# Gate logits from x1 and a premade grid product, long operations spread over the steps, and a block end of nine steps, in a GRU plus two-layer mixture kernel

## The chip, the core and the metric

The kernel runs on one core of a Trainium2 chip. A core has TensorE (PE), VectorE (DVE), ScalarE (ACT), GpSimd (POOL) and the queue of SyncE (SP), each with its own instruction stream; they meet by semaphores. The metric is the time of one execution on the device in microseconds (us), as the median of three runs.

## What is computed

A recurrence (GRU) runs over 512 time steps for a batch of four rows of width 512. Its states go through a mixture of eight LoRA experts, which gives x1. The second layer samples x1 along its width at the positions that a grid names (linear interpolation), routes each of the 2048 tokens to two of eight experts by a gate, and adds the experts' outputs to x1. Cut to what matters here:

```python
# layer 0: h_new = (1 - z) * n + z * h, step after step, then
base + einsum('ner,ne,eor->no', Ax, w_dense, lora_B) * SCALING
# layer 1, on x1 = x + layer 0
ix = (grid + 1.0) * 0.5 * (L - 1)
x0 = floor(ix);  w1 = ix - x0
x2 = (1 - w1) * x1[..., i0] + w1 * x1[..., i1]
logits = x2 @ gate_w.T + gate_b
top_vals, top_idx = top_k(logits, 2);  routing = softmax(top_vals)
for e in range(E):
    h = x2 @ w1[e].T + b1[e]
    y = x_glu * sigmoid(1.702 * x_glu) * (x_lin + 1.0)
    out = out + (y @ w2[e].T + b2[e]) * we[:, None]
```

## The kernel before

Every float32 operand of a product is split into two float16 parts, high and low, and each product is made of three matmuls (`PARTS`). ScalarE makes the high part, VectorE the low one (value times scale minus high part).

**Streams.** One recurrence step (`gru`) is a chain over the engines: PE multiplies the state's early part (L480), then its two parts (L486, L493) with `whh`; VectorE transposes and sums (L958 to L963), ScalarE takes the sigmoid, VectorE scans (L966), ScalarE takes the tanh, VectorE makes the new state (L972 to L977). The last instruction on `hs`, L977, ends the step; POOL's `keep` (L1261) copies the state away, and VectorE's next write of `hs` waits for that copy. Every engine's program is written by hand as: step, a piece of other work, step, a piece of other work. Which piece stands behind which step is what the tables at the top of the file say; no scheduler is involved.

**The parts of the program.** First a setup (weights loaded and split, input gates of the first 64 time steps). Then 128 steps whose other work is the *preparation* (`prelude`): `moe_hi` and `moe_lo` split 384 columns of expert weights per step on ScalarE and VectorE (L990), `gi_piece` makes input gates for later steps on PE (L503), `x_hi` and `x_lo` (L982) split inputs, `grid_op` makes the interpolation matrix `gm` for each batch row b and each quarter k of the width: g_d = position minus index (L1026), g_a = absolute value (L1028), ScalarE's hat function and its copy (`grid_hi`), and the low part (L1032); B x K = 16 of each. `GRID_AT` names their steps.

Then come four blocks f = 0 to 3 of 128 time steps each of the second half's work. Block f's work stands behind the recurrence steps of the next 128; the last block has no recurrence beside it (`gru_on` is false) and the same code runs without steps. A block is a *head* of `HEAD` = 30 steps, 15 expert tiles of `SLOT` = 6 steps and an *end* of 8 steps. The head, by step: LoRA products and first routing (0 to 5), base products (`base`, in pieces of `BASE_CUT`) and LoRA sums (`lora`, four calls in steps 6 and 9), x1 (L1107) and its split (L1112) in two halves, samples (`sample`, pieces of `SAMPLE_CUT`, 48 matmuls of 512 columns), the split of the samples x2 (L1119), their transpose (`turn_x2`, L543), gate logits from the transposed x2 (`gate`, L549), second routing (`route_a` to `route_c`), ranks (L556, L558), slots (L1126 to L1137), then four `scatter` calls on POOL (two indirect DMAs each, L1270) behind steps 23 to 26. At the end POOL gathers expert outputs (L1279) behind steps 122 to 125, ScalarE scales them, VectorE combines (L1166), PE transposes back and VectorE adds (L1161).

## Time and profile before

| what | us |
|---|---|
| median of 3 runs | 2033.37 (2032.92 to 2041.77) |
| profiled execution | 2053.76 |
| its span | 2051.9 |
| TensorE matmul busy | 1696.2 (83%) |
| VectorE busy | 1410.8 (69%) |
| ScalarE busy | 750.2 (37%) |
| POOL busy | 285.6 (14%) |
| mean granted TensorE clock | 0.966 |

The profiled execution is 20 us longer than the median, so a sum made on the trace is set against the execution's own time. The span is from the first to the last instruction of the trace. Busy shares are averages over parts with different limits: for 512 steps the chain of the recurrence sets the pace, in the last block the dependence of one product on the next.

### The profile page before, as it was taken

To read this page: it belongs to the slowest core of one execution; us is meant where nothing else is said; L and a number is where in the kernel's file an instruction comes from. 1 tells how busy PE (TensorE), PEld (TensorE's weight loads), DVE (VectorE), ACT (ScalarE), POOL (GpSimd) and SP (SyncE) were. 2 spreads that over 40 slices of the span, in tenths; PEclk is the share of its full clock that TensorE was granted. 3 is DMA by queue.
4 is the path that set the end of the run, shared out by engine and by line. 5 is a ranking of instruction groups with operands and counts; after the bars stand their busy time and mean duration, and the time that the engine had idled before them with its cause. 6 is when DMAs were issued, how large, how long until landed. Compare 5 with 4: busy or idle time off the path is not lost. (4 is left out here: it accounts for less than half of the span.)

```text
span 2051.9 us, 90285 instructions
## 1 busy us (share of the span) xinstructions
PE 1696.2 (83%) x38301; PEld 1095.2 (53%) x38301; DVE 1410.8 (69%) x6376; ACT 750.2 (37%) x2706; POOL 285.6 (14%) x581
## 2 busy tenths in 40 slices
PE   6777767778679999968599999978699999776995
PEld 4565555555445556545456566545456555442442
DVE  6888888887757777767677777767677777641221
ACT  5544444442323343322233343323233333322332
POOL 0111111121121111120211011120211111201001
PEclk9999999999989999999899999989899999987997
DMA  8444343422055464422265555240545464228995
GB/s 311 174 145 157 129 157 141 157 95 85 22 204 193 172 248 176 144 64 64 85 213 185 210 214 178 82 116 3 186 183 193 172 213 152 69 60 304 348 356 164
DMA packets 113621, 334.86 MB, mean 163 GB/s; under 512 B 41920, under 2 KB 42168, under 8 KB 100800
## 3 DMA queue, kind: packets, MB, share of 16 engines
q1 hardware_dynamic: 108096, 312.31, 42.8%
q0 software_dynamic: 5120, 16.78, 2.5%
q8 instruction: 299, 4.90, 1.0%
q14 instruction: 106, 0.87, 0.1%
HBM read 263.74 MB, written 65.32 MB: 160 GB/s over the span
## 5 line engine op out<-in xcount | busy, mean ns | idle before, releaser
L480 PE MATMUL bank_g<-whh,hs_early 128*32 128x256 f16 x8192 | 324.6, 279 | 257.7 <-DVE hs_early L972 247.9
L1261 POOL COPY hxs<-hs 128x32 f16<-128x32 f16 x512 | 221.7, 433 | 1519.6 <-DVE hs L977 1519.6
L727 ACT ACTIVATE rz<-pre 128x32 f32<-128x32 f32 x512 | 118.9, 232 | 804.2 <-DVE pre L960 804.2
L480 PEld LDWEIGHTS bank_g<-whh,hs_early 128*32 128x32 f16 x8192 | 173.8, 97 | 435.0 <-DVE hs_early L972 424.0
L958 DVE STREAM_TRANSPOSE xt<-bank_g 128x256 f32<-128x256 f32 x512 | 229.7, 449 | 201.8 <-PE bank_g L486 196.4
L626 PE MATMUL bank<-wm,wih 128*128 128x512 f16 x1440 | 351.1, 384 | 2.8 <-issue 1.6
L493 PE MATMUL bank_g<-whh,hs 128*32 128x128 f16 x16384 | 331.4, 222 | 6.6 <-issue 6.1
L486 PE MATMUL bank_g<-whh,hs 128*32 128x256 f16 x8192 | 321.6, 278 | 1.4 <-issue 1.1
L493 PEld LDWEIGHTS bank_g<-whh,hs 128*32 128x32 f16 x16384 | 290.5, 99 | 14.0 <-issue 10.3
L727 ACT ACTIVATE seq_h<-na 128x16 f32<-128x16 f32 x512 | 111.6, 218 | 283.2 <-DVE na L966 283.2
L486 PEld LDWEIGHTS bank_g<-whh,hs 128*32 128x32 f16 x8192 | 191.1, 98 | 43.5 <-DVE hs L977 3.3
L626 PEld LDWEIGHTS bank<-wm,wih 128*128 128x128 f16 x1440 | 126.9, 98 | 150.2 <-issue 20.9
L727 ACT ACTIVATE wih<-bank 128x512 f32<-128x512 f32 (+2 forms) x196 | 139.7, 713 | 132.5 <-PE bank L605 69.2
L972 DVE TENSOR_TENSOR_SCAN hs_early<-omz,seq_h 128x32 f16<-128x32 f32 x512 | 116.3, 227 | 103.3 <-ACT seq_h L727 102.9
L962 DVE STREAM_TRANSPOSE xt<-bank_g 128x128 f32<-128x128 f32 x512 | 157.8, 308 | 29.5 <-remote 17.7
L647 PE MATMUL bank<-wm,wih 128*128 128x512 f16 x720 | 173.1, 380 | 1.1 <-ACT wih L727 1.1
L503 PE MATMUL bank<-hxs,wih 128*128 128x256 f16 x1152 | 151.8, 278 | 18.2 <-DVE hxs L982 14.0
L960 DVE TENSOR_REDUCE pre<-xt 128x32 f32<-128x96 f32 x512 | 129.5, 253 | 17.6
L1149 DVE TENSOR_TENSOR wih<-bank,wih 128x512 f32<-128x512 f32 x60 | 41.2, 686 | 128.1 <-PE bank L622 128.1
L966 DVE TENSOR_TENSOR_SCAN na<-rz,seq_n 128x32 f32<-128x32 f32 x512 | 114.9, 224 | 18.8 <-DVE seq_n L963 0.8
L503 PEld LDWEIGHTS bank<-hxs,wih 128*128 128x128 f16 x1152 | 104.0, 99 | 44.0 <-DVE hxs L982 14.2
L727 ACT ACTIVATE xt<-gi 128x32 f32<-128x32 f32 x512 | 124.4, 243 | 0.0
(139 smaller groups left out, 1863.4 us busy)
## 6 DMA issues: line engine op xcount, KB each, us to landing
wm<-moe_split SPq DMA_DIRECT2D x60, 1536.0 KB
wm<-moe_split SPq DMA_DIRECT2D x60, 1024.0 KB
wm<-moe_split SPq DMA_DIRECT2D x60, 512.0 KB
wm<-in_w_moe SPq DMA_DIRECT2D x16, 1536.0 KB, 10.9
moe_split<-wm SPq DMA_DIRECT2D x16, 1536.0 KB, 6.4
wih<-x_rows SPq DMA_DIRECT2D x60, 256.0 KB, 7.6
y_rows<-wih SPq DMA_DIRECT2D x60, 256.0 KB, 4.9
xr<-in_x SPq DMA_DIRECT2D x16, 512.0 KB, 7.0
```

The lines of the kernel that those rows point to most:

```text
L480: mm(bank_g[0][32 * j:32 * j + 32, 0:2 * P], early_cols[:, 4 * B * k:4 * B * k + 32], whh[:, 1, k, at:at + 2 * P], start=(k == 0), stop=False)
L486: i = mm(bank_g[0][32 * j:32 * j + 32, 0:2 * P], hs_cols[:, 4 * B * k:4 * B * k + 32], whh[:, 0, k, at:at + 2 * P], start=False, stop=(k = ...
L493: i = mm(bank_g[1][32 * j:32 * j + 32, 0:P], hs_cols[:, 4 * B * k:4 * B * k + 32], whh[:, w, k, at:at + P], start=(k == 0 and w == 0), sto ...
L503: i = mm(bank[m % len(bank)][:, 0:N], wih[:, w, k, m * P:(m + 1) * P], xs[v % 2][:, a, k], start=(j == 0), stop=(j == len(GI) - 1))
L626: mm(bk[:, :], xgt[0][:, a, k], wm[:, par, at // HALF, w, up_at(at)], start=(c == 0), stop=False)
L647: mm(bank_down[:, :], yt[:, a, k], wm[:, par, 1, w, up_at(UPW + k * D)], start=(n == 0), stop=False)
L727: return nc.scalar.activation(dst, src, func, **kw)
L958: link(V.transpose(rows[:, 0:2 * K], bank_g[0][:, 0:2 * P].rearrange("p (m c) -> p m c", c=32)))
L960: V.tensor_reduce(pre[:, :, :], terms[:, 0:2 * K], AX, ALU.add).then_inc(S["rz_pre"], 1)
L962: link(V.transpose(rows[:, 2 * K:], bank_g[1][:, 0:P].rearrange("p (m c) -> p m c", c=32)))
L972: V.tensor_tensor_scan(early_scan, pairs["omz"], pairs["seq_h"], 0.0, ALU.mult, ALU.add).then_inc(S["h_hi"], 1)
L1261: Q.tensor_copy(hxs[:, par, :, :, :, col].rearrange("p s k b -> p s (k b)"), hs_new).then_inc(S["h_kept"], 1)
```

## The change

- **Gate logits.** Since x2 = x1 times the interpolation matrix G and logits = x2 times Wg, the product G times Wg can be made once. In the preparation PE transposes `gm` (`turn_grid`, 16 calls), ScalarE copies it out (`grid_out`), PE multiplies by `wgs` (`gate_grid`, 16 calls), and the result is split into `gws`. In the head `gate` then multiplies the split x1 (`x1s`) by `gws`, in steps 15 and 16. `turn_x2` and its copies go. `p_log`, `p_rank` and `p_count` move to another PSUM bank.
- **Samples.** The low part of x2 comes from PE and ScalarE instead of VectorE: `sub_hi` subtracts the high part from the bank by one matmul with `neg16`, and ScalarE copies what is left (`x2_lo`). The order of samples starts with rows 0 and 1 interleaved over k.
- **Head.** `lora`, x1, its high part and its low part each take one quarter per step (steps 7 to 10, 7 to 10, 8 to 11, 11 to 14). Second routing moves to steps 16 to 18, ranks to 19, slots to 19, expert numbers to 20, scatters to steps 20 to 23, each waiting for its own `x2_lo`. `HEAD` is 29.
- **Preparation.** The difference and absolute value of the grid become one `Abs` with a bias on ScalarE. All grid, x and other splits have hand-set steps, at most one long VectorE operation besides `moe_lo`. Input gates of the second visit start two steps later.
- **Setup.** The split of the second x piece, the split of b2, the 16-bit identity and the constants move from the setup into steps (`B2_AT`, `CONST_AT`). A one-element sigmoid (`warm`) stands at ScalarE's start.
- **Block end.** `TAIL` = 9 steps. Both pieces of the last `down` stand in the first of them. Gathers stand behind steps 121 to 124; `scaled`, `combined` and the last sum keep their steps.

The core of the diff:

```diff
-HEAD = 30
+HEAD = 29
+TAIL = 9
-SAMPLE = [(b, k, w, a) for b in range(B) for k in range(K) for w, a in PARTS]
-BASE_CUT = {2: (0, 8), 3: (8, 16), 4: (16, 24), 6: (24, 32), 7: (32, 40), 8: (40, 48)}
-SAMPLE_CUT = {11: (0, 6), 12: (6, 14), 13: (14, 22), 14: (22, 30), 15: (30, 39), 16: (39, 48)}
+SAMPLE = [(b, k, w, a) for k in range(K) for b in (0, 1) for w, a in PARTS] + \
+         [(b, k, w, a) for b in (2, 3) for k in range(K) for w, a in PARTS]
+BASE_CUT = {2: (0, 8), 3: (8, 16), 4: (16, 24), 5: (24, 26), 6: (26, 34), 7: (34, 38), 8: (38, 43), 9: (43, 48)}
+SAMPLE_CUT = {12: (0, 6), 13: (6, 12), 14: (12, 18), 15: (18, 19), 16: (19, 20), 17: (20, 27), 18: (27, 34),
+              19: (34, 41), 20: (41, 48)}
...
+GRID_START = (4, 26, 48, 70)
+X_LO = [s + q for s in (13, 21, 35, 53, 67, 89) for q in range(2)]
+GW_HI, B2_AT, B1_AT, CONST_AT = 104, 106, 110, 116
...
+            def sub_hi(f, b):
+                pe.wait_ge(S["x2_hi"], f * B + b + 1)
+                mm(bank[b][:, :], neg16[:, :], x2s[b][:, 0], start=False, stop=True, skip_group_check=True
+                   ).then_inc(S["x2_sub"], 1)
             def gate(f, b):
-                pe.wait_ge(S["x2t_out"], f * B + b + 1)
+                if b == 0:
+                    pe.wait_ge(S["x1_lo"], (f + 1) * K)
                 for j, (k, w, a) in enumerate(LOW):
-                    i = mm(p_log[:, b], xgt[b % 2][:, a, k], wgs[:, w, k], start=(j == 0), stop=(j == len(LOW) - 1))
+                    i = mm(p_log[:, b], x1s[:, a, k, b], gws[:, w, b, k], start=(j == 0), stop=(j == len(LOW) - 1))
...
             def last_down(f, i):
-                if i < 2:
-                    down(f, NT // 2, 0, 3 + i)
-                if i >= 4:
-                    b = i - 4
+                if i == 0:
+                    down(f, NT // 2, 0, 3)
+                    down(f, NT // 2, 0, 4)
+                if i >= 5:
+                    b = i - 5
...
+            def grid_abs(b, k):
+                act.wait_ge(S["grid_chain"], b * GRID_CHAIN + 2)
+                run(g_a, g_t, ACT.Abs, scale=-1.0, bias=iotf[:, k:k + 1]).then_inc(S["grid_a"], 1)
+            def x2_lo(f, b):
+                act.wait_ge(S["x2_sub"], f * B + b + 1)
+                run(x2s[b][:, 1], bank[b][:, :], ACT.Copy, scale=1 / WS).then_inc(S["x2_lo"], 1)
...
             def scatter(f, b):
                 if b == 0:
                     pool.wait_ge(S["slots_done"], f + 1)
-                    pool.wait_ge(S["x2_lo"], (f + 1) * B)
                     pool.wait_ge(S["xt_mm"], f * NT) if f else pool.wait_ge(S["zeroed"], 16 * NT)
+                pool.wait_ge(S["x2_lo"], f * B + b + 1)
```

How the order of instructions moves, at three places.

VectorE at the end of the setup, before. `whh` is the split of the recurrent weights, `xt<-bank_g` the first transpose of the first recurrence step.

```order
L1230 SCALAR_TENSOR_TENSOR whh<-wm,whh 128x4x32 x48
L982 SCALAR_TENSOR_TENSOR hxs<-xr,hxs 128x512 x2
L1236 SCALAR_TENSOR_TENSOR brow<-x1s,brow 8x512
L1238 MEMSET ones_f 128x128
L1239 MEMSET ones 128x128
L1240 MEMSET ones_as 128x128
L1241 SCALAR_TENSOR_TENSOR tri<-ones_f,idt 128x128
L1242 TENSOR_TENSOR tri<-tri,idt 128x128
L1243 COPY iott<-iote 128x8
L1244 TENSOR_SCALAR iott<-iote 128x8
L1245 TENSOR_SCALAR full<-iote 128x4
L958 STREAM_TRANSPOSE xt<-bank_g 128x256
```

The same place of the change:

```order
L1284 MEMSET ws_col 128x1
L1289 SCALAR_TENSOR_TENSOR whh<-wm,whh 128x4x32 x48
L1011 STREAM_TRANSPOSE xt<-bank_g 128x256
L1013 TENSOR_REDUCE pre<-xt 128x32
L1015 STREAM_TRANSPOSE xt<-bank_g 128x128
```

The eleven instructions between the split and the transpose are gone from here.

TensorE in the head of the last block, where no recurrence stands between, before. `gm,x1s` are samples, `id,wih` the transposes of x2, `wgs,wih` gate products, `both,tri` the first rank product.

```order
L524 MATMUL bank<-wih,wlb 128x512 x6
L532 MATMUL bank<-gm,x1s 128x512 x22
L543 MATMUL bank_l<-id,wih 128x128 x8
L532 MATMUL bank<-gm,x1s 128x512 x8
L549 MATMUL bank<-wgs,wih 128x8 x12
L532 MATMUL bank<-gm,x1s 128x512 x9
...
L549 MATMUL bank<-wgs,wih 128x8 x24
L556 MATMUL bank<-both,tri 128x8
```

The change; `gws,x1s` are gate products, `wih,neg` the subtraction of the high part.

```order
L527 MATMUL bank<-wih,wlb 128x512 x3
L535 MATMUL bank<-gm,x1s 128x512 x18
L549 MATMUL bank_l<-gws,x1s 128x8 x24
L535 MATMUL bank<-gm,x1s 128x512
...
L535 MATMUL bank<-gm,x1s 128x512 x8
L542 MATMUL bank<-wih,neg 128x512 x2
L535 MATMUL bank<-gm,x1s 128x512 x7
L556 MATMUL bank_l<-both,tri 128x8
```

The gate products stand behind 18 and 19 of the 48 samples instead of behind all of them, with 15 samples and two subtractions between them and the ranks.

TensorE at a block's end, before. `bank_g` rows are the recurrence of one step, `wm,wih` the last tile's `down`, `brow` its bias.

```order
L632 MATMUL bank_l<-id,wih 128x128 x8
L480 MATMUL bank_g<-whh,hs_early 32x256 x16
L486 MATMUL bank_g<-whh,hs 32x256 x16
L493 MATMUL bank_g<-whh,hs 32x128 x32
L647 MATMUL bank<-wm,wih 128x512 x5
...
L647 MATMUL bank<-wm,wih 128x512 x7
L644 MATMUL bank<-brow,ones_as 128x512
```

And of the change:

```order
L633 MATMUL bank_l<-id,wih 128x128 x8
L483 MATMUL bank_g<-whh,hs_early 32x256 x16
L489 MATMUL bank_g<-whh,hs 32x256 x16
L496 MATMUL bank_g<-whh,hs 32x128 x32
L648 MATMUL bank<-wm,wih 128x512 x12
L645 MATMUL bank<-brow,ones_as 128x512
```

Both pieces, 13 matmuls, stand behind one step of the recurrence where they stood behind two.

## Rows read from the trace of the kernel before

**Rows 1.** The page's costliest groups: line, engine, op; busy; idle before, releaser.

```profile
L480 PE MATMUL bank_g<-whh,hs_early 128*32 128x256 f16 x8192 | 324.6, 279 | 257.7 <-DVE hs_early L972 247.9
...
L727 ACT ACTIVATE rz<-pre 128x32 f32<-128x32 f32 x512 | 118.9, 232 | 804.2 <-DVE pre L960 804.2
...
L958 DVE STREAM_TRANSPOSE xt<-bank_g 128x256 f32<-128x256 f32 x512 | 229.7, 449 | 201.8 <-PE bank_g L486 196.4
```

**Rows 2.** Windows: us, busy PE, PEld, DVE, ACT, POOL, clock, DMA, GB/s.

```profile
39.50:477.30 437.80, 321.68 (x9232) 249.84 (x9224) 373.89 (x1614) 202.24 (x768) 82.14 (x128) 0.99 0.40 148
477.30:558.40 81.10, 64.56 (x1710) 44.34 (x1702) 62.29 (x313) 24.92 (x105) 7.62 (x23) 1.00 0.15 42
558.40:579.90 21.50, 8.58 (x260) 6.41 (x252) 9.52 (x47) 2.84 (x16) 9.28 (x12) 0.73 0.53 197
922.30:1004.80 82.50, 64.72 (x1712) 44.27 (x1702) 62.38 (x313) 24.92 (x105) 7.62 (x23) 1.00 0.17 44
1365.20:1445.50 80.30, 64.41 (x1714) 44.23 (x1702) 62.17 (x313) 24.91 (x105) 7.62 (x23) 1.00 0.18 46
887.30:922.30 35.00, 21.02 (x568) 15.88 (x560) 22.41 (x96) 9.19 (x37) 10.39 (x16) 0.90 0.28 78
1328.60:1365.20 36.60, 22.02 (x572) 16.16 (x560) 22.27 (x97) 9.09 (x37) 10.90 (x16) 0.81 0.27 74
1772.00:1803.40 31.40, 17.55 (x468) 12.79 (x456) 19.74 (x86) 8.23 (x31) 10.05 (x15) 0.89 0.27 78
```

**Rows 3.** Timeline of VectorE, preparation: start, duration, engine, line, operation.

```profile
309.31 0.19 DVE L977 TENSOR_TENSOR hs<-hh,hs_early 128x16 f16<-128x16 f32 x1
...
309.94 0.55 DVE L1026 TENSOR_SCALAR x<-x,iotf 128x512 f32<-128x512 f32 x1
...
312.66 0.19 DVE L977 TENSOR_TENSOR hs<-hh,hs_early 128x16 f16<-128x16 f32 x1
...
313.28 0.70 DVE L1028 SCALAR_TENSOR_TENSOR x<-x 128x512 f32<-128x512 f32 x1
...
316.16 0.19 DVE L977 TENSOR_TENSOR hs<-hh,hs_early 128x16 f16<-128x16 f32 x1
316.31 0.56 DVE L990 SCALAR_TENSOR_TENSOR wm<-wm 128x384 f16<-128x384 f32 x1
...
319.37 0.19 DVE L977 TENSOR_TENSOR hs<-hh,hs_early 128x16 f16<-128x16 f32 x1
```

**Rows 4.** Timelines of TensorE, ScalarE and VectorE at the end of the setup.

```profile
32.19 0.61 PE L486 MATMUL bank_g<-whh,hs 128*32 128x256 f16 x16
...
39.17 1.04 PE L480 MATMUL bank_g<-whh,hs_early 128*32 128x256 f16 x16 [3.56 <-DVE hs_early L972]
...
34.06 1.28 ACT L727 ACT_TABLE_LOAD   x1
...
37.08 0.45 DVE L958 STREAM_TRANSPOSE xt<-bank_g 128x256 f32<-128x256 f32 x1
```

**Rows 5.** Timeline of VectorE, the first block's head, steps 6 and 7.

```profile
497.11 0.19 DVE L977 TENSOR_TENSOR hs<-hh,hs_early 128x16 f16<-128x16 f32 x1
497.82 1.29 DVE L1107 SCALAR_TENSOR_TENSOR x<-bank,xr 128x512 f32<-128x512 f32 x2 [0.52 <-PE bank L524]
...
501.68 0.19 DVE L977 TENSOR_TENSOR hs<-hh,hs_early 128x16 f16<-128x16 f32 x1
502.36 1.23 DVE L1112 SCALAR_TENSOR_TENSOR x1s<-x,x1s 128x1024 f16<-128x1024 f32 x1 [0.49 <-ACT x1s L727]
```

**Rows 6.** Timelines of TensorE and POOL in the last block's head.

```profile
1825.03 3.63 PE L532 MATMUL bank<-gm,x1s 128*128 128x512 f16 x16 [1.84 <-DVE x1s L1112]
...
1838.62 0.46 PE L549 MATMUL bank<-wgs,wih 128*128 128x8 f16 x12 [0.83 <-ACT wih L727]
1841.16 0.18 PE L556 MATMUL bank<-both,tri 128*128 128x8 f16 x1 [2.08 <-DVE both L1123]
...
1843.75 1.02 POOL L1270 DMA_INDIRECT x_rows<-wih,slot_u  x1 [39.94 <-DVE slot_u L1137]
```

More of the change, by code:

```diff
@@ L900, in blk @@
                         slot(f, j // 2, j % 2, u, more=j + 1 < NT)
-                for i in range(FT - HEAD - NT * SLOT):
+                for i in range(TAIL):
                     step(HEAD + NT * SLOT + i)
@@ L906, in blk @@
                     gates_now((g + 1) * FT, 0)
+            act.wait_ge(S["warm"], 1)
+            run(warm, warm, ACT.Sigmoid)
             for q in range(3):
@@ L922, in _ @@
                     gi_out(0, m)
-            x_hi(1)
             act.wait_ge(S["bias_in"], 16 * 6)
-            run(b2_split[:, 0], b2f, ACT.Copy, scale=WS).then_inc(S["b2_hi"], 1)
             act.wait_ge(S["const_in"], 16 * 3)
-            run(id16[:, :], idt[:, :], ACT.Copy).then_inc(S["setup_act"], 1)
             act.wait_ge(S["gi_done"], G3)
@@ L1190, in blk @@
                         slot(f, j // 2, j % 2, u)
-                for i in range(FT - HEAD - NT * SLOT):
+                for i in range(TAIL):
                     step(HEAD + NT * SLOT + i)
```

346 lines of the change are left out of this document (187 added, 159 removed).

## The prediction

> **What bounds the kernel now.** I read the page's groups first. The first matmuls of a recurrence step wait 248 us in all for VectorE's state, VectorE's transposes wait 196 us for those matmuls, ScalarE waits 804 us for `pre` [rows 1]: the program is one serial chain of 512 steps, PE, DVE, ACT, DVE, PE, and other work is free as long as it fits the gaps. VectorE's timeline of the preparation shows the gap. The last instruction on `hs` (L977) marks a step. With the 0.56 us split of L990 alone beside the chain a step lasts 3.21 us (316.16 to 319.37): the floor. With a 0.55 us operation more it lasts 3.35 (+0.15), with a 0.70 us one more 3.50 (+0.30) [rows 3]. So VectorE has 0.56 + 0.70 - 0.30 = 0.96 us free per step. On TensorE the recurrence's three groups take some 1.45 (0.61 each, overlapping, [rows 4]) and a wide matmul (512 columns) 0.216 (16 in 3.63 us, [rows 6]): eight of them, 1.73, just fill the floor, each further one costs 0.22. ScalarE has the largest gap: 804 us over 512 steps is 1.6 us a step still unused [rows 1].
>
> The windows then say where the time above the floor is. The first 23 steps of the three blocks take 81.1, 82.5 and 80.3 us where 23 floors of 3.20 are 73.6; the last 8 steps of the first two take 35.0 and 36.6, the last 7 of the third 31.4, so 9.4, 11.0 and 9.0 above the floor [rows 2]. The last block has no recurrence: there the dependent chain itself counts.
>
> **Setup.** The first step's matmuls of L486 end at 32.8, but VectorE transposes them only at 37.08 [rows 4], behind two `x_lo`, the split of b2 and eight operations on constants. All of these move into steps (first pair of order rows); nothing is left between the weight split and the transpose. ScalarE's share (`x_hi`, `b2`, `id16`) moves too, so `now` is not late instead. Gain 37.1 - 32.85 = 4.2 (bounds 3.5 and 4.3). TensorE then idles shorter: before, it idled 3.56 us and came back at half clock, 16 matmuls in 1.04 us where 0.61 is usual [rows 4]. I count 1.0 for it (bounds 0 and 1.2, since steps 0 and 1 now carry no input matmuls).
>
> **Preparation, steps 0 to 127.** The 16 subtractions (L1026) and 16 absolute values (L1028) leave VectorE, at the prices of [rows 3]: 16 x 0.15 + 16 x 0.30 = 7.2 us. ScalarE gets 16 `Abs` in steps of their own, about 0.7 each as the like took on VectorE [rows 3], inside its 1.6: nothing. Added on VectorE: the doubled `x_lo` in step 1 (+0.9), b2's split (+0.3), constants in three steps (+0.8), 2.0 in all. Transposes of the grid (8 of 128 columns) or the 12 products of 8 columns stand beside seven input matmuls of 256 columns, half as wide as those that cost 0.22, some 1.4 us together, so TensorE's gap covers them; uncovered, the 32 steps would lose 2 us in all. Queues: SP loads x, grid and stages in other steps, each at least five steps (16 us) ahead of its use. Net 5.2 (bounds 3.0 and 7.2).
>
> No row shows an `Abs`. By the trace its price lies between nothing and two table loads of 1.28 us each, the only kind of switch that a row prices [rows 4]; I take nothing, since ScalarE's order has a single table load in the whole program, and `Relu` and `Copy` stood between sigmoids before.
> The Trainium skill (ScalarE: Activation LUTs, "Table sets: the hidden batching unit") says that abs is in every set, so that no load comes; the same page ("What ACT_TABLE_LOAD costs") puts a switch at 2.66 us. An estimate by that figure for 32 switches would take up to 85 us from the gain; no run here shows it.
>
> **Head of a block, three times.** Before, step 6 holds 14 wide matmuls and two sums (1.29 us), before which VectorE idles 0.52 for PE: it lasts 4.57 (497.11 to 501.68). Step 7 holds a 1.23 us split that waits 0.49 for ScalarE [rows 5]. Steps 10, 11 and 13 to 16 repeat the pattern; in the third block, the cleanest, the sum is 6.7 above the floor [rows 2]. After: steps 7 to 14 have one 0.7 us operation on VectorE, whose input was made a step before, and at most eight wide matmuls (0.2 in all); steps 1 to 3, 16 and 17 keep their routing (0.3); step 18 has nine wide matmuls (+0.3); step 19 has all eight small operations from `over` to `slot_u`. In the last block that piece and the rank products take 1841.16 to 1843.75, 2.6, of which I put 1.8 on VectorE [rows 6]: 1.8 - 0.96 = +0.9. That makes 1.7. Gain 6.7 - 1.7 = 5.0 per block, 15.0 in all (bounds 9 and 17; the second block's 2 us more than the third's stay, since no long operation makes them). The four scatters move from steps 23 to 26 to steps 20 to 23. Such a step lasts 21.5 / 4 = 5.4 [rows 2], 2.2 above the floor, wherever it stands: no change. `keep` is queued behind each on POOL and VectorE's next `hs` behind that; a scatter now waits for its own `x2_lo`, which ScalarE makes a step or more ahead.
>
> **Block end, three times.** HEAD of 29 and the ninth end step put the last `down` into one step: 12 wide matmuls and the bias row, 13 where it was 5 and 8. That is 5 x 0.22 more than eight, +1.1 (third pair). Gathers start one step earlier while `scaled`, `combined` and the final sum stay in their steps. The stalls under the gathers so cover one step less of those with two sums on VectorE (1.3 as L1107's pair [rows 5], less 0.96: +0.4), while ScalarE's wait for a late gather, by which I explain the second block's 11.0 against 9.0 [rows 2], goes: 0.6 on average. Net -0.9 a block, -2.7 in all (bounds -5.4 and 0).
>
> **Last block.** Before, gate products end at 1839.1, since they need every sample, its split and a transpose; ranks start at 1841.16, the scatter at 1843.75 [rows 6]. After (second pair): the x1 splits end at 1825.0 as before, when the samples resume [rows 6], but in four pieces of 0.61 (half of 1.23, [rows 5]), the first at 1823.2. 18 samples run to 1827.1, 48 gate products (12 take 0.46) and one sample to 1828.9. Up to the ranks PE still has 17 wide matmuls, 3.7 us, longer than the routing, 2.1 (1839.1 to 1841.16). Ranks at 1832.6, scatter at 1832.6 + 2.6 = 1835.2. Gain 8.5 (bounds 7 and 9.5). All that follows starts on the scatter's landing and shifts with it; expert weights are asked for as much earlier.
>
> **Sum.** 4.2 + 1.0 + 5.2 + 15.0 - 2.7 + 8.5 = 31.2 us. The profiled execution took 2053.8 (span 2051.9 and 1.9 around it), so 2022.6 like for like. The median of the runs is 2033.4; off the same 31.2 it gives 2002.
>
> **Rivals.** (1) The heads keep much of their excess: it moves from long operations to the nine-matmul step, the chain of step 19 and the hand-over of x1 splits. For it: step 19 does lengthen. Against it: the shares of PE and VectorE fit by the order. With 9 instead of 15 and the ends at their worst: 2002 + 6 + 2.7 = 2011. (2) The gate chain is hardly shortened, because samples and sub products stand ahead of the ranks and wait for ScalarE's copies: the last block gains 3, time 2007.5. (3) More than forecast: gathers a step earlier take all waits out of the block ends and the other terms reach their good bounds: 1994. (4) Slower: TensorE falls to half clock in the thinned heads, with six wide matmuls or fewer in steps 10 to 16 where it had up to nine and transposes. At half clock each of a step's three recurrence groups costs 0.43 more (1.04 against 0.61, [rows 4]), some 1.2 us a step. With 14 steps (10 to 23) in each of three heads: 42 x 1.2 = 50, 2052. From 35 such steps on it is slower than before by over 0.5%: (2043.5 - 2002) / 1.2. Against it: all three head windows were granted 1.00 [rows 2], though their steps 17 to 22 hold next to nothing but the recurrence.
>
> **Numbers.** Forecast 0.72 (1994 to 2010), rival 1 0.13, rival 2 0.06, rival 3 0.06, rival 4 0.03. The terms' low bounds add up to 17 (2016), their high ones to 39 (1994); the range is 1994 to 2013. A difference of under 0.5% (10 us, from 2023 on) is about what a measurement of this kernel can't tell from no change. Faster by more: nearly all of the first four cases, 0.93. Within: 0.04, when the low bounds meet one unseen cost. Slower by more: 0.03, rival 4.
>
> **What would show it.** The first `hs` ends at 35.3 instead of 39.5. The preparation's steps take some 432 us instead of 437.8. In heads, steps 6 to 16 stand within 0.1 of the floor and step 19 at about 4.1; the 20 steps before the first scatter take 66 us. The step of the last `down` takes 4.3. In the last block 8.5 us less lie between its start and the first scatter. It would be wrong if the granted clock fell below 1.00 in heads, if steps with `Abs` stood above the floor, if VectorE waited for ScalarE in steps 11 to 14, or if POOL waited for `x2_lo`.

## The result, and where the time went

The changed kernel takes 1976.6 us (median of four, 1972.2 to 1980.3) where the kernel before takes 2037.2 beside it: a ratio of 0.970, 95% interval 0.967 to 0.974. The forecast was 2002, range 1994 to 2013. The sign is right; the gain is 60 us where 31 was expected, and the time lies outside the range.

The profiled execution took 1980.3, its span is 1978.5. These are the groups of its page that answer to [rows 1] (line, engine, op; busy, mean ns; idle before, releaser):

```profile
L483 PE MATMUL bank_g<-whh,hs_early 128*32 128x256 f16 x8192 | 321.1, 276 | 209.1 <-DVE hs_early L1025 198.0
...
L750 ACT ACTIVATE rz<-pre 128x32 f32<-128x32 f32 x512 | 119.0, 232 | 763.1 <-DVE pre L1013 763.1
...
L1011 DVE STREAM_TRANSPOSE xt<-bank_g 128x256 f32<-128x256 f32 x512 | 229.9, 449 | 202.2 <-PE bank_g L489 195.5
```

It is the same serial chain. And the windows that answer to [rows 2] (us; busy PE, PEld, DVE, ACT, POOL; granted clock, DMA share, GB/s): preparation, the first head up to its scatters, its four scatter steps, the second and third head, and the last nine, nine and eight steps of the three blocks.

```profile
36.40:473.70 437.30, 334.42 (x9557) 265.96 (x9545) 362.59 (x1593) 228.82 (x806) 81.66 (x128) 0.99 0.41 150
473.70:540.20 66.50, 59.23 (x1489) 38.19 (x1481) 52.92 (x278) 19.91 (x94) 8.16 (x20) 1.00 0.19 53
540.20:554.10 13.90, 7.06 (x261) 5.32 (x256) 9.42 (x48) 3.85 (x19) 9.28 (x12) 0.90 0.82 289
900.10:965.80 65.70, 59.06 (x1493) 37.98 (x1481) 53.04 (x278) 19.95 (x94) 8.17 (x20) 1.00 0.21 55
1322.40:1388.30 65.90, 59.17 (x1493) 37.98 (x1481) 53.08 (x278) 19.99 (x94) 8.16 (x20) 1.00 0.21 55
868.40:900.10 31.70, 18.91 (x637) 14.84 (x634) 24.09 (x108) 9.35 (x41) 11.53 (x17) 1.00 0.30 86
1290.70:1322.40 31.70, 19.02 (x637) 14.79 (x634) 23.97 (x108) 9.41 (x41) 11.45 (x17) 1.00 0.30 86
1712.10:1740.50 28.40, 15.47 (x532) 11.82 (x530) 21.25 (x96) 8.47 (x35) 11.14 (x16) 1.00 0.30 86
```

The heads came as forecast: 20 steps in 66.5, 65.7 and 65.9 where 66 was written. The surprise is beside them. The four scatter steps took 21.5 at a clock of 0.73 [rows 2] and take 13.9 now; in the second and third block they take 13.1 and 13.0. The block ends stood 9.4, 11.0 and 9.0 above the floor [rows 2]; now 9 x 3.2 = 28.8 against 31.7, and 8 x 3.2 = 25.6 against 28.4, so 2.9, 2.9 and 2.8. The preparation, forecast at 432, takes 437.3 where it took 437.8: in sum nothing came of it.

So 24 steps in which GpSimd issues two indirect transfers each, four scatters and four gathers a block, seem to have lost their 2.2 us. Nothing in the change says why. The stall itself looks like this in the kernel before (timeline, the first scatter step):

```profile
558.91 0.62 PE L493 MATMUL bank_g<-whh,hs 128*32 128x128 f16 x32
...
559.30 1.16 POOL L1270 DMA_INDIRECT x_rows<-wih,slot_u  x1 [0.50 <-issue]
...
560.76 0.97 POOL L1270 DMA_INDIRECT x_rows<-wih,slot_u  x1 [0.30 <-issue]
...
562.38 0.32 DVE L962 STREAM_TRANSPOSE xt<-bank_g 128x128 f32<-128x128 f32 x1 [2.50 <-remote]
```

And the same place of the changed kernel's second block:

```profile
966.33 0.62 PE L496 MATMUL bank_g<-whh,hs 128*32 128x128 f16 x32
...
966.63 1.02 POOL L1316 DMA_INDIRECT x_rows<-wih,slot_u  x1 [0.42 <-issue]
...
967.30 0.32 DVE L1015 STREAM_TRANSPOSE xt<-bank_g 128x128 f32<-128x128 f32 x1
...
967.96 0.97 POOL L1316 DMA_INDIRECT x_rows<-wih,slot_u  x1 [0.31 <-issue]
```

Both times TensorE's 32 products of the second group are under way when GpSimd begins. In the first trace VectorE, idle since 559.88, gets them only at 562.38, 0.65 us after GpSimd's second row ends (560.76 + 0.97 = 561.73), though the products' own row ends at 559.53. The view gives the releaser as "remote" and names no instruction. In the second trace VectorE goes on at once. (The ends of matmul rows are modelled, so a product that is held does not show on its own row; VectorE's wait does.)

### The profile page after: what moved, and what is told of

Same layout as the page of the kernel before. It is cut to its first block and busy times, and to the rows that moved or that the text cites. A ratio compares the mean times of both kernels' runs of the same rounds, so it can differ in the third digit from the quotient of the medians.

```text
span 1978.5 us, 90744 instructions
## 1 busy us (share of the span) xinstructions
PE 1683.3 (85%) x38509; PEld 1087.5 (55%) x38509; DVE 1382.4 (70%) x6337; ACT 766.0 (39%) x2748; POOL 292.6 (15%) x582
## 5 line engine op out<-in xcount | busy, mean ns | idle before, releaser
L1307 POOL COPY hxs<-hs 128x32 f16<-128x32 f16 x512 | 226.5, 442 | 1450.7 <-DVE hs L1030 1450.5
L496 PE MATMUL bank_g<-whh,hs 128*32 128x128 f16 x16384 | 323.5, 220 | 9.3 <-issue 9.1
L489 PE MATMUL bank_g<-whh,hs 128*32 128x256 f16 x8192 | 315.8, 274 | 1.2 <-issue 0.9
L496 PEld LDWEIGHTS bank_g<-whh,hs 128*32 128x32 f16 x16384 | 284.5, 97 | 14.4 <-issue 12.1
L489 PEld LDWEIGHTS bank_g<-whh,hs 128*32 128x32 f16 x8192 | 188.1, 97 | 41.3 <-DVE hs L1030 2.9
L750 ACT ACTIVATE wih<-bank 128x512 f32<-128x512 f32 (+2 forms) x212 | 148.0, 703 | 127.7 <-PE bank L606 63.3
```

The costliest lines, as they stand in the source:

```text
L489: i = mm(bank_g[0][32 * j:32 * j + 32, 0:2 * P], hs_cols[:, 4 * B * k:4 * B * k + 32], whh[:, 0, k, at:at + 2 * P], start=False, stop=(k = ...
L496: i = mm(bank_g[1][32 * j:32 * j + 32, 0:P], hs_cols[:, 4 * B * k:4 * B * k + 32], whh[:, w, k, at:at + P], start=(k == 0 and w == 0), sto ...
L750: return nc.scalar.activation(dst, src, func, **kw)
L1307: Q.tensor_copy(hxs[:, par, :, :, :, col].rearrange("p s k b -> p s (k b)"), hs_new).then_inc(S["h_kept"], 1)
```

## Experiments: what holds the products

The step times below are worked out from each trace: a step lasts from one end of the last `hs` instruction to the next, the piece of other work behind recurrence step k runs in step k, and the excess is what a step lasts above 3.20.

**Not numbering, not placement, not the tables.** Three versions of the kernel before, each with one thing that the change moves without meaning to.

```diff
-            setup_dve setup_act wih_hi
+            setup_dve setup_act spare_sem wih_hi
```

> The kernel before with one unused semaphore declared ahead of the GRU's, so that the semaphore TensorE raises for a finished gate moves from number 123 to 124, where the changed kernel has it; no instruction differs. Question: why TensorE's gate products are late (by up to 2.8 us) while GpSimd issues its two indirect transfers in the kernel before, and are not in the changed one, though the instructions around are the same. Theory N (numbering decides): the 24 steps with indirect transfers fall from 5.4 to 3.2 to 4.2 us, time 1985 to 1995. Theory W (work of head and tail decides, say where the steps stand or what TensorE did before) and theory P (placement in the on-chip memory): no change, 2033 to 2042.

```diff
         ws_col = sb("ws_col", [P, 1], F32)
+        pad_a = sb("pad_a", [P, 2, B, K, E], F16)
+        pad_b = sb("pad_b", [P, P], F16)
+        pad_c = sb("pad_c", [P, 1], F32)
```

> The kernel before with three unused tiles declared after its last one, of the sizes of the changed kernel's three new tiles (gws, neg16, warm_col), so that whatever the compiler places behind the kernel's tiles moves as it did with the change; no instruction differs. Theory P (placement decides): the 24 steps with indirect transfers fall to 3.2 to 4.2 us, time 1985 to 1995. Theories N and W: no change, 2033 to 2042.

```diff
+            act.wait_ge(S["warm"], 1)
+            run(pre[:, 0, 0:1], pre[:, 0, 0:1], ACT.Sigmoid).then_inc(S["warm"], 1)
...
+            Q.memset(pre[:, 0, 0:1], 0.0).then_inc(S["warm"], 1)
```

> The kernel before with the changed kernel's first act alone: GpSimd sets one column to zero and ScalarE takes a Sigmoid of it before its first weight split, so that the table is loaded there once. Theory S (the state of ScalarE's tables left by the start decides about the stalls under the indirect transfers): 1985 to 1995. Theories N, P and W: only the table load of 1.3 us and perhaps 1 us more leave the start, 2031 to 2041, the 24 steps at 5.4.

They took 2056.9, 2055.6 and 2054.6 beside 2054.3 for the kernel before, with ratios of 1.0005, 0.9999 and 0.9998, each with an interval of 0.2% around it, and the scatter steps stay at 5.2 to 5.9. None of the three does anything here. All three times miss the level that was written for "no change" (2033 to 2042), because the kernel before itself takes 2054 here. That theories N, P and S are out altogether follows only from two runs further down: the changed kernel, with all three things in it, has the stall (a_again), and the kernel before, with none of them, is seen without it (b_chip2).

**The place of the scatters.**

```diff
-                steps(0, 20)
+                steps(0, 23)
                 for b in range(B):
-                    steps(20 + b, 21 + b)
+                    steps(23 + b, 24 + b)
                     scatter(f, b)
-                steps(20 + B, end + 2)
+                steps(23 + B, end + 2)
```

> The changed kernel with the four scatters of a block back in steps 23 to 26, three steps later, as in the kernel before; all else as changed. My prediction held that a step with two indirect transfers costs 2.2 us extra wherever it stands. Theory W in the form that the distance to TensorE's last filler work decides (two to six steps with gate products alone before the scatters let it stall): the four steps of each block go to about 5.4, +26 us in all, 2000 to 2006. Theories N, P and S: they stay at 3.2 to 4.2, 1975 to 1985 (up to 1.5 us per block more if the first tile's rows land late).

It took 2033.0, more than any theory gave, and steps 23 to 26 lasted 5.2 to 5.5 as theory W wanted. But the gathers' steps, which had not moved, were back at 4.8 to 5.5 too. And the kernel before took 2054.3 on this chip, not 2037. That made the chip a suspect, and the unaltered changed kernel was run beside three more versions.

> The changed kernel once more, unaltered, beside the kernel before and the three below. With its scatters three steps later it took 2033 where 1977 stood for it, and even its gathers, which had not moved, stalled again (steps of 5.2 instead of 3.2 to 3.6 us). Theory C (the chip that a run falls on decides whether TensorE waits while GpSimd issues indirect transfers): on a chip where the kernel before takes about 2054, this one takes 2025 to 2030, with 24 steps at 4.8 to 5.5. Theory W (the place of the scatters decides): 1972 to 1980 wherever it runs.

The same three lines as above with 21 in the place of 20:

> The changed kernel with the scatters one step later, in steps 21 to 24. Theory W (two or more steps of gate products alone before the first scatter bring the stall): part of the loss, 1990 to 2010. Theory C: like the unaltered changed kernel on the same chip, within 4 us.

The kernel before with 22 in the place of 23:

> The kernel before with the scatters one step earlier, in steps 22 to 25, straight behind the step in which the row numbers are made. Theory W: some of the stalls go, 2035 to 2050 where the kernel before takes 2054. Theory C: no change beside the kernel before on the same chip, within 4 us.

And `end + 3` for `end + 2` in the gathers of the changed kernel:

> The changed kernel with the gathers one step later, in steps 122 to 125 as in the kernel before; the four turns back then wait for them, 0 to 3 us more per block. Theory W for the gathers: their steps go to 5.2, +6 us per block, 1992 to 2000 in all, the scatter steps unchanged. Theory C: like the unaltered changed kernel on the same chip, 0 to 9 us more for the later rows alone.

The changed kernel took 2024.0 here, beside 2056.7 for the kernel before: a ratio of 0.984, interval 0.981 to 0.987. Single runs of the others gave 2020.1 (a_21), 2060.7 (b_22) and 2030.6 (a_g1). The changed kernel is 1 us under theory C's range, the other three lie within what it gave them, and theory W has nothing left to explain: in every one of them the 24 steps take 4.8 to 5.9, wherever they stand, but for one of 4.0 in a_21 and a pair of 3.3 and 8.9 in b_22's second block end (explained further down). The changed kernel's three scatter windows and its first block end on this chip:

```profile
538.20:560.10 21.90, 9.59 (x261) 6.79 (x257) 9.50 (x48) 3.86 (x19) 9.27 (x12) 0.75 0.52 194
978.90:1000.60 21.70, 9.45 (x264) 6.84 (x256) 9.47 (x47) 3.79 (x18) 9.14 (x12) 0.75 0.54 196
1417.30:1439.10 21.80, 9.97 (x265) 7.40 (x257) 9.53 (x48) 3.85 (x19) 9.13 (x12) 0.69 0.53 194
874.10:913.20 39.10, 23.11 (x637) 17.79 (x634) 24.36 (x108) 9.35 (x41) 11.51 (x17) 0.83 0.25 70
```

These are the 21.5 at 0.73 of [rows 2] again, now in the changed kernel, at steps 20 to 23.

**What GpSimd does in them.** A busy GpSimd without indirect transfers, and the same transfers at another time of the step.

```diff
-                    Q.indirect_dma_start(x_rows, bass.IndirectOffsetOnAxis(ap=slot_u[:, b, c:c + 1], axis=0),
-                                         unit(7 + b), None).then_inc(S["scattered"], 16)
+                    if f + b + c:
+                        pool.wait_ge(S["scattered"], ((f * B + b) * 2 + c) * 16)
+                    Q.memset(unit(3), 0.0).then_inc(S["scattered"], 16)
```

> The changed kernel without its scatters (the experts' input rows stay zero, 1 MB per block is not written): in the place of each indirect transfer GpSimd sets a tile of 128x1024 to zero, 0.95 us each, so it is as busy as before. Theory D (making descriptors for an indirect transfer, or its traffic, stalls TensorE): the 12 scatter steps fall to 3.2 to 3.4, some 27 us less than the changed kernel on the same chip. Rival G (GpSimd busy, or waiting, is enough): the steps stay at 5.2 to 5.5, no change.

Ahead of each pair of transfers, `t` being the step just kept:

```diff
+                if t is not None:
+                    pool.wait_ge(S["gates_mm"], (t + 1) * 2 + 2)
```

> The changed kernel with one wait more on GpSimd: in the steps with indirect transfers it issues them only when TensorE's gate products of the step are done (some 1.2 us after the step's hs), while VectorE and ScalarE work through the gates. Theory H (TensorE cannot finish a product from the issue of an indirect transfer until 0.65 us after its descriptors are made, so what counts is how much of these 2.9 us lies on the gate products): the second group is free, only the next step's first products lie under the tail; steps of 3.4 to 4.3 instead of 5.2 to 5.5, 24 of them: 25 to 45 us less, 1980 to 2000 beside 2055 of the kernel before, or no change where the changed kernel takes 1977. Rival T (the transfers' traffic, or the wait itself, keeps TensorE from finishing, whenever they are issued): the stall moves with them, 2015 to 2035.

The same two lines in the kernel before:

> The same wait in the kernel before. Theory H: 25 to 45 us less than the kernel before on the same chip (2010 to 2030 beside 2055). Rival T: within 5 us of it, or slower.

And with `+ 1` in the place of `+ 2`, in the changed kernel:

> As a_gate, but GpSimd waits for TensorE's first group of gate products of the step instead of the second. In a_gate the transfer began 0.75 us after the second group was done and its tail held the next step's first products by 1.0 us (steps of 4.2). Begun 0.45 us earlier, still behind the second group, the tail should reach 0.45 us less far. Theory H: steps of 3.6 to 3.9 instead of 4.2, 24 of them: 8 to 14 us less than a_gate's 1998, 1984 to 1990. Rival: the second group is caught again by the transfer's beginning, steps of 4.5 or more, 2005 to 2025.

On a chip where the kernel before takes 2057.6, a_busy, which leaves out the scatters, took 1993.7 in its one run. That is 30 us less than the changed kernel's 2024.0 on another stalling chip, where theory D gave 27. Its scatter windows:

```profile
540.20:553.20 13.00, 6.43 (x269) 5.02 (x257) 9.24 (x47) 3.81 (x18) 8.54 (x12) 1.00 0.46 165
970.70:983.80 13.10, 6.31 (x269) 5.04 (x257) 9.21 (x47) 3.79 (x18) 8.53 (x12) 1.00 0.44 165
1398.70:1411.70 13.00, 6.43 (x269) 5.04 (x261) 9.34 (x48) 3.86 (x19) 8.53 (x12) 1.00 0.44 165
```

GpSimd is busy for 8.5 of the 13 us as before (9.3), yet the clock is 1.00 and no step is long, while the gathers of the same run, left as they were, still cost 10.4, 9.8 and 11.6 above the floor. Rival G is out: it is the indirect transfer, not a busy GpSimd. Whether it is the making of its descriptors or its traffic this run can't tell, since both are gone.

a_gate took 1997.9 beside 2057.6, a ratio of 0.970 (0.968 to 0.973), where the unaltered changed kernel had 0.984. Theory H's mechanism, in a timeline of a_gate:

```profile
976.48 0.31 DVE L1015 STREAM_TRANSPOSE xt<-bank_g 128x128 f32<-128x128 f32 x1
...
976.89 0.98 POOL L1318 DMA_INDIRECT x_rows<-wih,slot_u  x1 [1.56 <-PE bank_g L496]
...
977.92 0.62 PE L483 MATMUL bank_g<-whh,hs_early 128*32 128x256 f16 x16 [1.79 <-DVE hs_early L1025]
978.18 0.96 POOL L1318 DMA_INDIRECT x_rows<-wih,slot_u  x1 [0.30 <-issue]
...
979.69 0.62 PE L496 MATMUL bank_g<-whh,hs 128*32 128x128 f16 x14 [0.44 <-issue]
979.83 0.45 DVE L1011 STREAM_TRANSPOSE xt<-bank_g 128x256 f32<-128x256 f32 x1 [1.54 <-PE bank_g L489]
```

The second group is through before the transfers begin. The next step's products are issued at 977.92, but VectorE gets the first group at 979.83: 0.69 after GpSimd's second row ends (979.14). The hold is the same as above (0.47 to 0.87 behind the second row in the steps of this run whose first group is held); only less of it lies on the chain. A step costs 4.0 to 4.4 instead of 5.2 to 5.8. In sum the steps 20 to 28 of the three blocks fell from 29.3 to 16.1 above the floor, the ends from 32.1 to 16.4.

a_gate1 took 1995.6 beside 2056.1 (0.970, 0.968 to 0.972), 6 us above the forecast of 1984 to 1990, and its ratio is that of a_gate: the earlier start gained nothing that can be measured. The scatter steps fell in part (3.5 to 4.3 where 3.6 to 3.9 was written), and in the block ends four steps stand at the rival's 4.5 or more (5.4, 5.8, 4.6, and 4.9 in the second block). In one of them the transfer began at 880.04 and VectorE, idle since 880.54, got the second group at 882.17. That is the rival, in part of the 24 steps.

b_gate is the telling miss: 2056.6 beside 2057.6, ratio 0.9995 (0.998 to 1.001), no gain at all. The time is the one that rival T gave, but the steps are not: the stall did shrink, and the steps that the transfers reach (24 to 27) took 3.7 to 4.4. But step 28, which turns the first tile's rows, took 6.6, 6.7 and 8.2 instead of 3.2 to 3.9, the step of the first combined gather (123) 8.2, 7.7 and 7.6, and step 125 7.6 to 8.8. When the stall shrinks, waits for the rows come up that it had covered.

## Experiments: a chip that spares the stall

Four chips gave the kernel before 2054 to 2058. The first comparison had 2037. So the unaltered kernels were profiled beside the later runs as well, on the chips that these fell on.

> The kernel before, unaltered, for its profile on this chip. Two chips so far gave it 2054 and 2057 with 24 stalled steps of 5.2 to 5.5. Theory C (the chip decides on the stalls): where its median is 2033 to 2041, the stalled steps are shorter, 4.2 or less on average; where it is 2050 or more they are as in the profile shown, 5.2 to 5.5.

> The kernel before, unaltered, for its profile on the chip of this call. Theory C (chips differ in the stall): if before's median here is 2045 or less, its 24 steps take 4.3 or less on average; if it is 2050 or more they take 5.2 to 5.5. Theory K (the changed kernel alone is spared there): at a median of 2033 to 2041 before's steps still take 5.2 to 5.5 and the 17 us are missing elsewhere.

Both fell on stalling chips, those of a_gate and of a_gate1: 2055.7 and 2058.7, the steps mostly 5.2 to 6.0 (in the second block's end one gather step of 8.4 to 8.5 takes the place of two). The next chip was of the other kind:

> The kernel before, unaltered, for its profile on the chip of this call. Theory C (the chip decides on the stalls): median 2045 or less goes with 24 steps of 4.3 or less on average, 2050 or more with 5.2 to 5.5. Theory K (only the changed kernel is spared): at 2033 to 2041 before's steps still take 5.2 to 5.5.

> The changed kernel, unaltered, on the chip of this call, for its profile beside before's. Where before takes 2050 or more: 2020 to 2028, 24 steps of 4.8 to 5.5. Where before takes 2033 to 2041: 1972 to 1981, steps of 3.2 to 4.3.

| chip | before, median | changed, median | ratio | indirect steps |
|---|---|---|---|---|
| first comparison | 2037.2 | 1976.6 | 0.970 (0.967 to 0.974) | not held (changed) |
| stalling, pair on one chip | 2056.7 | 2024.0 | 0.984 (0.981 to 0.987) | held |
| three more stalling ones | 2054.3, 2057.6, 2056.1 | not run | | held |
| sparing, pair on one chip | 2037.7 | 1979.7 | 0.971 (0.968 to 0.974) | not held (both) |

The sparing chip spares both kernels: the scatter steps of the kernel before took 3.2 to 3.4 there but for one of 4.3, and theory K is out. Theory C's 4.3 on average over 24 steps is met with 4.2, but the 12 gather steps stand at 5.1 in it, for another reason. "Chip" is what theory C calls it; each call ran on one chip and no chip came twice, so something else that stays the same during a call would look alike. That the stall is a matter of where a kernel runs and not of the kernel is shown; what there makes it is open.

Some 50 us of stalls (24 times 2.1) turned into only 17 to 20 us of time. Where the rest stays shows in its windows: scatter steps 23 to 26 and steps 27 and 28 of the first block, and that block's last eight.

```profile
557.40:571.50 14.10, 6.30 (x264) 4.96 (x260) 9.28 (x48) 2.84 (x16) 9.28 (x12) 1.00 0.81 288
...
571.50:581.80 10.30, 6.38 (x153) 4.22 (x145) 4.37 (x23) 2.45 (x9) 0.65 (x2) 0.83 0.65 210
880.90:916.60 35.70, 22.03 (x568) 16.59 (x560) 22.21 (x97) 9.09 (x37) 10.71 (x16) 0.81 0.30 83
```

The first is free of stalls. The second is 10.3 for two steps: step 28 takes 7.0 (7.9 and 8.0 in the other blocks). Its timeline names the wait, and so does that of the gathers:

```profile
573.82 0.35 SPq L417 DMA_DIRECT2D wih<-x_rows  x1
...
576.56 0.65 PE L605 MATMUL bank<-id,wih 128*128 128x128 f16 x8 [3.88 <-DMA wih<-x_rows]
```

```profile
888.33 0.99 POOL L1279 DMA_INDIRECT xr<-y_rows,slot_u  x1 [0.44 <-issue]
...
895.59 0.75 DVE L1166 SCALAR_TENSOR_TENSOR xr<-x1s,tpr,xr 128x512 f32<-128x512 f32 x1 [4.79 <-ACT xr L727]
896.26 0.44 DVE L958 STREAM_TRANSPOSE xt<-bank_g 128x256 f32<-128x256 f32 x1
```

The last scatter is issued at 568.92 (step 26). SP, which waits for the scatters to land, asks for the first tile's rows at 573.82, and TensorE has them at 576.56, 7.6 us after the issue; it stood in front of them for 3.9, with the recurrence behind it. Likewise the first gather, issued at 888.33 in step 122, lets VectorE add it at 895.59, 7.3 us later, in step 123: a wait of 4.8 with the recurrence's transpose queued behind. In the steps behind it the half clock (0.62 and 0.52 granted at 899 to 902 and 908 to 911) and two waits of 1.0 for later gathers add more. At 3.2 us a step the kernel before puts too few steps between issue and use; at 5.3 us a step, with the stall, they fit.

One place of the stalling profile from which the forecast was made shows the same wait. In its second block end the first gather waits for the experts' output, is issued at 1337.05, late enough to miss the step's products, and step 122 takes 3.2. Then:

```profile
1344.28 0.75 DVE L1166 SCALAR_TENSOR_TENSOR xr<-x1s,tpr,xr 128x512 f32<-128x512 f32 x1 [5.88 <-ACT xr L727]
```

That is 7.2 us after the issue, and step 123 takes 9.0. The b_again and b_chip1 steps of 8.4 to 8.5 are at the same place. The changed kernel scatters in steps 20 to 23 and turns rows a step earlier, which leaves two steps more; it gathers in steps 121 to 124 and adds from 123 on, which leaves one more. On the same chip its steps 27 and 28 take 3.2 to 3.4 (steps 23 to 26 of its first block 4.2 at half clock, without a stall; more on that at the end), and its ends stand 2.8 to 2.9 above the floor: the last `down` (4.4) and three or four steps with two sums (3.6).

**The early table load.**

```diff
-            act.wait_ge(S["warm"], 1)
-            run(warm, warm, ACT.Sigmoid)
```

> The changed kernel without the early Sigmoid: the table load of 1.28 us goes back to its first use. By the forecast's setup term it is worth 1.3 us of the 4.2: the first hs ends 1.3 us later and the whole kernel is 0 to 2 us slower than the changed kernel on the same chip. Rival: ScalarE loads its table while it waits for the first weights anyway, so nothing changes, within 0.5 us.

1976.3 (1972.7 to 1978.5) on the sparing chip, beside 1979.7 for the changed kernel: no loss that can be measured. The end of the first `hs`, at 35.0, settles nothing, since it lies between 34.6 and 36.4 in nine profiles with the changed kernel's setup. The rows of the first step tell more:

```profile
32.15 1.28 ACT L750 ACT_TABLE_LOAD   x1
33.45 0.23 ACT L750 ACTIVATE rz<-pre 128x32 f32<-128x32 f32 x1
33.78 0.22 DVE L1017 TENSOR_TENSOR_SCAN na<-rz,seq_n 128x32 f32<-128x32 f32 x1 [0.46 <-ACT rz L750]
```

From VectorE's first transpose (32.12) to the end of `hs` it is 2.89 us, against 2.46 (33.92 to 36.38) in the changed kernel. So most of the load runs while ScalarE waits and 0.4 us of it is on the chain: the rival's "within 0.5" is right, its "nothing changes" and the forecast's 1.3 are not. In the kernel before VectorE was busy with constants until 37.08, and there taking the load away (b_warm) gained nothing.

## Why the prediction was wrong, and where it was right

The terms of the forecast beside the same parts of the traces. "Stalling" sets the profile of before, from which I worked, against the changed kernel's on a stalling chip (spans 2051.9 and 2024.3); "sparing" is the pair on the sparing chip (2031.7 and 1980.6). Setup and last block scatter between executions of one kernel: the first `hs` ends at 34.6 to 36.4 in the profiles with the changed setup, and the last block of the kernel before lasts 246.0 to 248.5 in its four, that of the changed kernel 238.0 to 240.5 in its three. A difference of one or two us between the two columns means nothing there.

| part | forecast | stalling | sparing |
|---|---|---|---|
| setup, to the end of the first `hs` | -4.2 | -4.3 | -3.0 |
| first step's clock, and preparation | -6.2 | -0.6 | +1.1 |
| heads, steps 0 to 19, three | -15.0 | -16.5 | -15.1 |
| steps 20 to 28, three | 0 | -1.8 | -10.9 |
| steps 29 to 118, three | 0 | +3.4 | +2.0 |
| ends, steps 119 to 127, three | +2.7 | +2.6 | -18.9 |
| last block | -8.5 | -10.3 | -6.4 |
| span | -31.2 | -27.6 | -51.1 |

**Like for like it was nearly right.** The forecast for a profiled execution of 2053.8 was 2022.6; on a chip that gives such executions the changed kernel's median is 2024.0. Heads (step 19 at 4.0, first 20 steps at 66), the step of the last `down` (4.4 where 4.3 was written) and the ends' small loss came as worked out, setup too. Part of the near hit is luck: the preparation is 5.6 short and the middle of the blocks 3.4, and heads, steps 20 to 28 and last block make up for 5.1. Of rivals 1, 2 and 4 nothing is to be seen: heads gained 16.5 and 15.1 and not 9, 10.5 were gained up to the last block's scatter, and every head's window is granted 1.00.

**The step that failed** is the last one of the sum: "The median of the runs is 2033.4; off the same 31.2 it gives 2002." The 20 us between the profiled execution and the median were noted, and not asked about. They are the difference between a chip that holds the products under an indirect transfer and one that doesn't, and that difference changes what the change is worth. With it falls the sentence that a scatter step costs 2.2 above the floor "wherever it stands: no change". It was true of the stall. But nothing was said of what the stall hides: 7.6 us from a scatter's issue to the row in TensorE's reach, 7.3 from a gather's issue to the sum, both shorter than the steps between them mostly because those steps are long. (The one place where the gather's was bare, step 123 of the second block, was read as a late gather and priced at 0.6 a block.) On the sparing chip these latencies are bare in the kernel before, and the rescheduling, which I priced at nothing for the scatters and at a loss for the gathers ("gathers start one step earlier" was there, at 0.6 a block), takes them away: 10.9 + 18.9 us, where I had +2.7. Rival 3 had half of it, that gathers a step earlier take all waits out of the block ends, with a chance of 0.06 and 8 us for it and all other terms at their good bounds. Take these two rows out and the other five sum to -21.4 there, against -33.9 forecast; the 12.5 lacking are the preparation (7.3), the setup (1.2), the last block (2.1) and the middle of the blocks (2.0), of which setup and last block are within what executions of one kernel differ by.

That the two latencies are the cause on the sparing chip rests on its timelines and on four other places where a shorter stall, a missing one or a later scatter brought the same waits: b_gate's step 28, a_late's step 27 (7.3 to 7.5, where the changed kernel turns its rows), b_gate's step 123 and step 123 of the second block in the profile of before. For the scatter a_late is the test, since it moves nothing else; for the gather no run moved it alone on a sparing chip. That the first comparison ran on a sparing chip is an inference: its medians (2037.2 and 1976.6) and its changed profile are those of the sparing chip; a profile of before was not taken there.

**Preparation: 5.2 forecast, and in sum nothing gained.** The operations left VectorE as counted: its busy time in the window fell from 373.9 [rows 2] to 362.6. Most steps paid for it. Without steps 0 and 1 and the four steps 42, 51, 58 and 99, the preparation stood 22.1 us above the floor before and stands 17.2 above it now: 4.9 gained, where the terms for these steps make 6.1 (7.2 less the 1.1 for b2 and the constants). The nine profiles of the kernel before and its variants have 21.5 to 23.0 here and the ten of the changed one 17.2 to 18.0, so this part is no accident. It is taken back in two places.

The first is four steps, at 4.8, 4.8, 6.2 and 5.6. Together they stood 4.9 above the floor and now stand 8.5 above it (4.2 to 6.7 in the nine profiles, 8.0 to 10.4 in the ten). In each TensorE stops. Step 51 (its timeline):

```profile
208.05 0.62 PE L496 MATMUL bank_g<-whh,hs 128*32 128x128 f16 x32
210.89 0.38 PE L506 MATMUL bank<-hxs,wih 128*128 128x256 f16 x2 [2.21 <-issue]
```

"issue" says that it waited for nothing the profile shows. The stops are 1.28, 2.21, 2.34 and 2.17 us long; in the kernel before they were 0.57, none, 2.45 and 0.30. The DMA view of 208.6 to 209.8 has, in the row of the instruction queue, one packet of 16 KB, beside a load that fills the engines (share of 16 engines in the last column):

```profile
q1 hardware_dynamic: 42, 0.52, 103.5%
q8 instruction: 1, 0.02, 5.1%
```

Such a packet starts within 0.3 us of the stop in steps 51, 58 and 99, and in step 58 of the kernel before as well. It may be that TensorE ran out of instructions there; but some 300 such packets come in an execution, most without a stop, step 42's stop has none beside it, and no run here takes that apart. The cause stays open. The forecast had no term for it.

The second is the start. Step 1 has the doubled `x_lo` and takes 4.1, as forecast. Step 0, for whose clock I had 1.0, lasts 4.2 in both kernels. TensorE does come back at full pace (16 matmuls in 0.61 to 0.62 where it was 1.04 [rows 4]), but ScalarE has the moved `x_hi` and identities ahead of its weight split, and VectorE waits for that split with the transpose queued behind:

```profile
37.68 0.56 DVE L1043 SCALAR_TENSOR_TENSOR wm<-wm 128x384 f16<-128x384 f32 x1 [1.30 <-ACT wm L750]
```

So ScalarE's share of what was moved out of the setup, put at nothing, took back what the clock gave.

VectorE's waits tell how much of the work taken off it TensorE would have covered anyway. From 45 to 450 us (us in total, times, longest), before:

```profile
DVE hs_early L972 <- ACT seq_h L727: 23.3, 117, 0.2
DVE xt L958 <- PE bank_g L486: 15.9, 46, 2.7
```

and after:

```profile
DVE xt L1011 <- PE bank_g L489: 24.4, 69, 3.0
DVE hs_early L1025 <- ACT seq_h L750: 24.2, 118, 0.6
```

Of the 8.5 us more of waiting for TensorE half, 4.3, is in the four steps. The other half is spread over the rest, where TensorE is now the one waited for in some 20 steps more; there it cost the forecast no more than the 1.2 between 6.1 and 4.9.

**Last block.** 18 samples start 18.2 us after the block's first instant (1740.45), ranks at 27.2, the scatter at 29.8:

```profile
1758.68 4.06 PE L535 MATMUL bank<-gm,x1s 128*128 128x512 f16 x18 [1.38 <-DVE x1s L1179]
...
1767.67 0.17 PE L556 MATMUL bank_l<-both,tri 128*128 128x8 f16 x1
...
1770.24 1.02 POOL L1316 DMA_INDIRECT x_rows<-wih,slot_u  x1 [29.40 <-DVE slot_u L1196]
```

Before, the scatter came 40.3 after it (1843.75 [rows 6] less 1803.5), so 10.5 were gained to this point where 8.5 was forecast. The pieces have the sizes of the forecast (18 samples 4.06 for 3.9, ranks to scatter 2.6 for 2.6); the samples' start, put at 19.7, was 1.5 too late. Over the whole block 10.3 remain in the stalling pair and 6.4 in the sparing one. Executions of one kernel differ by 2.5 us in this block, so these two values show a gain near the forecast's 8.5 and not more.

## What to carry over

Before a gain worked out on one profile is taken off a median, the two must be of the same kind: 20 us between them was a question, and its answer was worth as much as the change. A stall that seems to belong to the machine is also cover: for each one, work out what latency it hides, and price moves that lengthen the distance between issue and use by that latency, not by what waits today. And a window that shows no gain may hold a gain and a loss: here the long operations taken off VectorE paid in most steps, and four stops of TensorE and one wait for ScalarE took it back. Compare the two kernels step by step before calling a term wrong.

Of the runs, a_gate and a_gate1 are faster than the changed kernel on stalling chips (0.970 of before where that has 0.984, in each case beside the kernel before on the same chip). They were not run beside the changed kernel on one chip, nor on a sparing one; there is no stall there to avoid, and no run shows what the later issue costs.

## What the runs showed of the hardware

- While GpSimd issues indirect transfers (0.98 us each, two with 0.3 between), TensorE's products don't reach VectorE, on the four stalling chips. Where VectorE waits, it mostly gets them 0.5 to 0.85 us after the second row ends (0.65 in the first stall shown), or it gets one group 1.0 to 1.15 after the first row ends and waits again for the next. In the four profiles without the stall its waits for the second group are at most 0.07 us in the scatter steps, but for one step in the first block of the changed kernel in which TensorE itself stops (0.42 us of "issue" in the first profile). A memset of 0.98 us in its place holds nothing (a_busy). In GpSimd's own rows the chips don't differ: 1.02 and 0.97 us for a pair on either. What in the chip differs is open.
- The half clock follows the stall and doesn't cause it: in the first stall of the profile of before the wait ends at 562.38; the granted clock is 1.00 from 559.0 to 562.3, 0.98 from 563.8 to 564.9 and 0.50 from 564.9 to 565.9. Over the four scatter steps it is 0.69 to 0.75 with the stall [rows 2], 1.00 in a_busy without it. But it can fall without a stall too. In the first block of the changed kernel's first profile TensorE was busy 1.50 us in each of steps 21 and 22 (543.5 to 549.9) at 1.00. In step 23 it stopped for 0.42 us, was granted 0.66 (549.9 to 554.1) and then 0.50 (554.1 to 558.3), and steps 23 to 25 took 4.0 to 4.3. The same steps of the second and third block were as little busy without the stop, kept 1.00 and took 3.2.
- The Trainium skill (SBUF — State Buffer, "SBUF: two separate sides") says that within the engine side "only the shared port pair causes contention" and that TensorE never waits on anyone; the lock it describes is one between VectorE and GpSimd. The sparing chip's traces agree (waits of at most 0.07 us, as above). On the four stalling ones VectorE waits up to 2.5 us for TensorE's products while GpSimd issues (2.50 in the first stall), so either the rule has an exception or it isn't the port that holds them; no run here tells which.
- A table load on ScalarE takes 1.28 us in every trace. At the end of the setup it costs 0.4 us in a_nowarm, where VectorE is ready for ScalarE, and nothing in the kernel before, where VectorE is not. The next activation starts 0.02 us behind it (33.45 after 32.15 + 1.28).
